# Slot-mean prologue moved ahead of the first statistics, PSUM copies of the transposes shared by two engines, and two waits merged

## The reference

```python
xn = layernorm(x)
# first branch: a gated scan along the tokens
w, k = (xn @ Wp + bp) split;  u = xn @ Wu + bu
gate = sigmoid(w);  s = gate * (s * tanh(k) + u) + (1 - gate) * s   # per token
attn = s_all @ Wo + bo
# second branch: 64 slots
slot_mean = mean of the 64 rows of slot_init (same for all tokens)
h = gelu(concat(xn, slot_mean) @ w1 + b1)
logits = (h @ w2 + b2) / (abs(tau) + 0.1)
alpha = softmax over the 8 largest of 64 logits, scattered back to 64
slot_input = alpha^T @ xn, summed over all tokens   # then a GRU, an attention
slot_values = ...                                   # over 64 slots, a layernorm
out = x + attn + (alpha @ slot_values) @ wo + bo
```

## Time and profile before

| | us |
|---|---|
| median of two runs | 1833.52 (1829.3 and 1837.74) |
| the profiled execution | 1837.19 |
| its span, from the slowest core's first to last instruction (core 6) | 1835.6 |
| spans of the eight cores | 1795.5 to 1835.6 |
| PE busy on core 6 | 1543.7 (84%) |
| DVE busy | 751.2 (41%) |
| ACT busy | 568.3 (31%) |

### The profile page before, as it was taken

One profiled execution on the slowest core, in us unless ns is written; L12 is line 12 of the kernel. 1 busy time (PEld: TensorE's weight loads), 2 busy tenths in 40 slices (PEclk: granted clock), 3 DMA queues, 4 the chain that ended last, 5 costly groups with the idle time before them and its releaser, 6 DMA issues.

```text
span 1835.6 us, 21069 instructions; the slowest of 8 cores (1795.5 to 1835.6 us)
## 1 busy us (share of the span) xinstructions
PE 1543.7 (84%) x7221; PEld 677.0 (37%) x7221; DVE 751.2 (41%) x1359; ACT 568.3 (31%) x926; POOL 26.9 (1%) x54
## 2 busy tenths in 40 slices
PE   0198999999999999999999899898844369999998
PEld 0044444444444444444444444444311123333333
DVE  0235444464554645546455464554501112222222
ACT  0252424244253352523525235252101121111110
POOL 0100000000000000000000000000011000000000
PEclk9999878899999999989989999999956669989898
DMA  9622020202202022021230302201199345545545
GB/s 152 152 46 92 1 92 1 92 2 91 92 1 92 24 69 92 1 92 37 57 92 1 92 34 60 92 1 47 53 151 168 60 128 207 202 184 192 198 184 206
DMA packets 42680, 166.52 MB, mean 91 GB/s; under 512 B 4290, under 2 KB 5458, under 8 KB 41682
## 3 DMA queue, kind: packets, MB, share of 16 engines
q1 hardware_dynamic: 36178, 134.29, 21.1%
q0 software_dynamic: 6400, 30.89, 10.2%
HBM read 128.68 MB, written 67.11 MB: 107 GB/s over the span
## 4 chain that ended last, share of the span: by engine, by line
PE 72%; DMA 10%; DVE 9%; issue 4%; DVEq 3%; ACT 2%; ACTq 0%; SPq 0%; POOL 0%; POOLq 0%
PE psA L1042 7%; PE psA L437 6%; PE psC L449 6%; PE psC L442 6%; PE psA L442 6%; PE psB L449 6%; PE psB L437 6%; PE psA L511 4%; PE psA L299 4%; PE psC L1042 3%; PE psB L1042 3%; PE psB L511 3%; DMA sb_bq_c<-bq_pk 2%; DVEq L102 2%; DMA sb_WT<-Wih_pk 2%
## 5 line engine op out<-in xcount | busy, mean ns | idle before, releaser
L19 ACT ACT_TABLE_LOAD x83 | 106.5, 1283 | 402.0 <-PE psA L511 398.2
L481 DVE SCALAR_TENSOR_TENSOR sb_a_sb<-sb_g_sb,sb_s_sb 128x512 f32<-128x512 f32 x128 | 88.6, 692 | 290.3 <-PE psB L449 157.2
L493 DVE TENSOR_TENSOR_SCAN sb_ys_bf<-sb_a_sb,sb_ys_bf,sb_b_sb 128x512 bf16<-128x512 f32 x120 | 154.1, 1284 | 8.9
L1042 PE MATMUL psA<-sb_wo_sb,sb_z_f 128*128 128x512 bf16 x512 | 138.6, 432 | 20.5 <-ACT sb_z_f L1011 18.8
L1057 DVE TENSOR_TENSOR sb_prd<-psA,sb_prd 128x1024 f32<-128x1024 f32 x32 | 39.2, 1224 | 258.6 <-DMA sb_prd<-out 171.1
L437 PE MATMUL psA<-sb_xn_f,sb_Wp_sb 128*128 128x512 bf16 x512 | 125.8, 390 | 0.0
L299 PE MATMUL psA<-sb_Wo_sb,sb_ys_bf 128*128 128x512 bf16 x512 | 121.3, 386 | 4.7 <-DVE sb_x_sl L327 4.7
L442 PE MATMUL psC<-sb_xn_f,sb_Wp_sb 128*128 128x512 bf16 x512 | 124.0, 386 | 0.0
L442 PE MATMUL psA<-sb_xn_f,sb_Wp_sb 128*128 128x512 bf16 x512 | 124.0, 386 | 0.0
L437 PE MATMUL psB<-sb_xn_f,sb_Wp_sb 128*128 128x512 bf16 x512 | 124.0, 386 | 0.0
L449 PE MATMUL psB<-sb_xn_f,sb_Wu_sb 128*128 128x512 bf16 x512 | 124.0, 386 | 0.0
(11 more groups left out here) (224 smaller groups left out, 1900.3 us busy)
## 6 DMA issues: line engine op xcount, KB each, us to landing
sb_x_sl<-x SPq DMA_DIRECT2D x32, 1024.0 KB, 7.4
out<-sb_x_sl SPq DMA_DIRECT2D x32, 1024.0 KB, 4.1
sb_prd<-out SPq DMA_DIRECT2D x16, 2048.0 KB, 10.5
out<-sb_prd SPq DMA_DIRECT2D x32, 1024.0 KB, 4.6
sb_WT<-Wih_pk POOLq DMA_DIRECT2D x12, 512.0 KB, 8.7
sb_whh_pp<-Whh_pk POOLq DMA_DIRECT2D x12, 512.0 KB, 8.6
sb_Wp_sb<-Wp_pk POOLq DMA_DIRECT2D x1, 4096.0 KB, 31.5
sb_Wu_sb<-Wu_pk POOLq DMA_DIRECT2D x1, 2048.0 KB, 37.8
```

The lines of the kernel that those rows point to most:

```text
L19: return eng.add_instruction(mybir.InstLoadActFuncSet(name=eng.bass.get_next_instruction_name(), act_func_set_id=idx, ins=[], outs=[]))
L481: P.op("ve", lambda v, pp=pp: v.scalar_tensor_tensor(t.a_sb[:], t.g_sb[:, pp, :], -2.0, t.s2_sb[:, pp, :], ALU.mult, ALU.mult))
L493: P.op("ve", lambda v, j=j, init=init: v.tensor_tensor_scan(t.ys_bf[:, j, :], t.a_sb[:], t.b_sb[:], init, ALU.mult, ALU.add), inc="sve", e ...
L1042: P.op("pe", lambda e, i=i, f=f, k=k, ps=ps, p2=p2: e.matmul(ps[:, f * 512:(f + 1) * 512], t.z_f[:, p2 % 2, k, i * 128:(i + 1) * 128], t.w ...
```

## The change

It has four parts.

1. The whole block for the slot mean (with its eight loads, and the three weight loads behind it) moves from behind `ln_apply(0)` to ahead of `stats_tile(0, ...)`. On DVE it so stands before `var_chain(0)`; on PE its place is the same.
2. In `xn_transposes` the blocks with odd `k` are copied by ACT with an Identity activation, those with even `k` still by DVE. PE waits for the last block of each engine.
3. In `wku_loop` the event `wk` is gone: ACT waits for `wku`, all 24 matmuls of the round, before its two sigmoids. DVE drops its own wait for `wku`.
4. In `h_logits` PE waits for the last of the four gelus before the first of the small matmuls; it waited for each of them in turn.

```diff
 (the block of L597 to L649, unchanged, now stands ahead of stats_tile)
...
-            P.wait("ve", ("xnT", ph, k))
+            eng = "ve" if k % 2 == 0 else "se"
+            P.wait(eng, ("xnT", ph, k))
             if ph >= 1 and k < 2:
-                P.wait("ve", ("wku", ph - 1, ND - 1))
-                P.wait("ve", ("hmm", ph - 1, NH - 1))
-            P.op("ve", lambda v, k=k, psT=psT: v.tensor_copy(
-                t.xn_f[:, k, :], psT[:, 0:Tp]), inc="sve", event=("xnf", ph, k))
+                P.wait(eng, ("wku", ph - 1, ND - 1))
+                P.wait(eng, ("hmm", ph - 1, NH - 1))
+            if k % 2 == 0:
+                P.op("ve", lambda v, k=k, psT=psT: v.tensor_copy(
+                    t.xn_f[:, k, :], psT[:, 0:Tp]), inc="sve",
+                    event=("xnf", ph, k))
+            else:
+                P.op("se", lambda s, k=k, psT=psT: s.activation(
+                    t.xn_f[:, k, :], psT[:, 0:Tp], AF.Identity), inc="sse",
+                    event=("xnf", ph, k))
...
     def wku_loop(ph):
         P.wait("pe", ("xnf", ph, ND - 1))
+        P.wait("pe", ("xnf", ph, ND - 2))
...
-                    t.xn_f[:, k, :], start=(k == 0), stop=(k == ND - 1)),
-                    inc="spe" if last else None,
-                    event=("wk", ph, j) if last else None)
+                    t.xn_f[:, k, :], start=(k == 0), stop=(k == ND - 1)))
...
-            P.wait("se", ("wk", ph, j))
+            P.wait("se", ("wku", ph, j))
...
             P.wait("ve", ("gs", ph, j))
-            P.wait("ve", ("wku", ph, j))
...
     def h_logits(ph):
         P.wait("pe", ("xnf", ph, ND - 1))
+        P.wait("pe", ("xnf", ph, ND - 2))
...
+        P.wait("pe", ("hf", ph, NH - 1))
         pe_claim("C0")
         for i in range(TPT):
             for kh in range(NH):
-                if i == 0:
-                    P.wait("pe", ("hf", ph, kh))
```

More of the change, by code:

```diff
@@ L206, in build_walk @@
         out=t.bo_tot[:], in_=t.bo1_r[:]), "sg", event=("botot",))
+    P.wait_all_dma("pe", ("cload",), "sx")
+    P.wait_all_dma("pe", ("wload",), "sg")
+    pe_claim("T0")
+    for k in range(ND):
+        P.op("pe", lambda e, k=k: e.transpose(
+            t.psT0[:, k * 64:(k + 1) * 64],
+            t.s0_bf[0:64, k * 128:(k + 1) * 128], t.ident[0:64, 0:64]),
+            inc="spe" if k == ND - 1 else None,
+            event=("s0T",) if k == ND - 1 else None)
+    P.wait("ve", ("s0T",))
+    for k in range(ND):
+        P.op("ve", lambda v, k=k: v.tensor_copy(
+            t.si0f[:, k, :], t.psT0[:, k * 64:(k + 1) * 64]),
+            inc="sve" if k == ND - 1 else None,
+            event=("si0f",) if k == ND - 1 else None)
@@ new lines, in build_walk @@
+    release("T0", ("si0f",))
+    P.drain("ve")
+    for k in range(ND):
+        P.op("ve", lambda v, k=k: v.reduce_sum(
+            t.sm_f[:, k:k + 1], t.si0f[:, k, :], axis=AX.X))
+    P.drain("ve")
+    P.op("ve", lambda v: v.tensor_scalar(t.sm_fb[:], t.sm_f[:], 1.0 / 64.0, None,
+                                         ALU.mult), inc="sve", event=("smf",))
+    regs4 = ["A0", "A1", "B0", "B1"]
+    pe_claim(*regs4)
+    ps4 = [psH[r] for r in regs4]
+    for k in range(ND):
+        if k >= 2:
+            P.wait("gp", ("smwk", k - 2))
+        P.dma("gp", lambda g, k=k: g.dma_start(
+            out=t.w1s[:, k % 2, :],
+            in_=t.i_w1[1024 + k * 128:1024 + (k + 1) * 128, :]), "sg",
+            event=("w1s", k))
+        P.wait("pe", ("w1s", k))
+        if k == 0:
+            P.wait("pe", ("smf",))
+        for jh in range(NH):
+            P.op("pe", lambda e, jh=jh, k=k: e.matmul(
+                ps4[jh][:, 0:1], t.w1s[:, k % 2, jh * 128:(jh + 1) * 128],
+                t.sm_fb[:, k:k + 1], start=(k == 0), stop=(k == ND - 1)),
+                inc="spe" if jh == NH - 1 else None,
+                event=("smwk", k) if jh == NH - 1 else None)
@@ L208, in stats_tile @@
+    P.wait("ve", ("smwk", ND - 1))
+    for jh in range(NH):
+        P.op("ve", lambda v, jh=jh: v.tensor_add(
+            t.bias_h[:, jh:jh + 1], t.b1_c[:, jh:jh + 1], ps4[jh][:, 0:1]),
+            inc="sve" if jh == NH - 1 else None,
+            event=("biash",) if jh == NH - 1 else None)
+    for r in regs4:
+        release(r, ("biash",))
+    for i, fn in enumerate(gload2):
+        P.dma("gp", fn, "sg", event=("wload2",) if i == len(gload2) - 1 else None)
     def stats_tile(ph, i):
@@ L440, in wku_loop @@
             for k in range(ND):
-                last = (k == ND - 1)
                 P.op("pe", lambda e, j=j, k=k, psk=psk: e.matmul(
                     psk, t.Wp_sb[:, k, 1024 + j * 128:1024 + (j + 1) * 128],
-                    t.xn_f[:, k, :], start=(k == 0), stop=(k == ND - 1)),
-                    inc="spe" if last else None,
-                    event=("wk", ph, j) if last else None)
+                    t.xn_f[:, k, :], start=(k == 0), stop=(k == ND - 1)))
             for k in range(ND):
@@ L596, in build_walk @@
     ln_apply(0)
[L598 to L649, removed]
     for ph in range(NPH + 1):
```

## The result

The changed kernel takes 1860.97 us (median), against 1835.78 us for the kernel before in the same comparison. The ratio is 1.018, with an interval of 1.013 to 1.022: slower by 1.8%, as forecast, and at the border of what counts as within 2%. The forecast time was 1867. In three of the eleven executions of the changed kernel one die ran at a lower granted clock and the time was 1974 to 2076 us; the ratio leaves such executions of either kernel out.

The account below looks back on a forecast made before the run. PE, busy 84% of the span, was taken as the bound, with DVE ending its wait before tile 3. Terms 18.2 + 9.6 + 1.8 + 6.3 - 2.0 gave +33.9 us, hence 1867 us; 8-in-10 range 1849 to 1884.

Parts of the forecast that it names:

- The late gates: In `wku_loop`, later sigmoids delay DVE's last round and so tile 3 of `wo_block`: 1.4 us in 13 phases, 18.2 us.
- The copies: In `xn_transposes`, the T1 chain goes through the slower ACT: 0.6 us a phase, 9.6 us in all (7 to 13.4).
- the faster reaction of PE to ACT: In `xn_transposes`, PE starts 0.14 us after ACT ends against 0.25 us after DVE's addition, lowering the price of ACT's copies.
- The gelus: In `h_logits`, three more small matmuls follow the wait for gelu 3: 0.11 us a phase, 1.8 us in all.
- The prologue: Before phase 0, slot-mean block and statistics change places without overlapping: a gain of 2 us (bounds 0 and 5).
- The clock: From slot matmuls to first L511, a longer pause makes 3 of 4 full-speed phases lose the clock: 6.3 us (0 to 16).
- the longer pause: Slot matmuls to first L511 gets some 0.6 us longer, given as the reason that more phases lose the full clock.
- The sum: For core 6: 18.2 + 9.6 + 1.8 + 6.3 - 2.0 = +33.9 us, 1867.4 against the median, 1.8% slower.
- The low-clock phases don't come back: Rival: without core 6's two slow phases the slowest core resembles core 1, 1810 + 42 = 1852 us; chance 0.12.
- the trace agrees, with 12 falls in 16: Before the first L511, 12 of core 6's 16 groups were slow, taken to support that transposes don't count as busy time.

Follow-up runs that it names:

- the gates alone: The kernel before with only both sigmoids made to wait for all three matmul groups of the round; ratio 1.010, median span 1833.8 us.
- part 1 alone: The kernel before with only the slot-mean block moved ahead of the statistics; one profiled execution, median span 1810.2 us.
- the copies alone: The kernel before with only the odd blocks of the transposes copied by ACT; ratio 1.010, median span 1834.4 us.
- an altered order: The changed kernel with DVE running `ln_apply` of the next phase behind the addition of tile 1, not the last scan; ratio 1.013 to the kernel before.
- the pause filled: The changed kernel with 13 extra unread matmuls a phase between the transposes; ratio 1.011 to the kernel before, median span 1831.9 us.

## Why the prediction was right, and what in it was not

**The late gates: right.** 1.4 us a phase forecast, 1.48 measured (22.2 us over 15 phases; 21.9 with the gates alone). The path was the one named: last sigmoids, DVE's last round, `ln_apply`, the addition of tile 0, tile 3. The regions of round 7 and the last scan held nobody. What was too small is the count: 13 phases were taken, because two were at low clock on core 6. The profiled run of the changed kernel had no such phases, and all 15 paid. Not foreseen was that the longer wait before tile 3 can itself be a place for falls: 19 with the gates alone, none in the changed kernel.

**The copies: right in mechanism, a little low.** 0.6 us a phase, between 0.4 and 0.84; measured 0.72 to 0.73. The copy took less than the nearest row: 597 ns, where 629 ns had been taken from rows 8. From the groups by line and shape:

```profile
L480 ACT ACTIVATE sb_xn_f<-psT 128x512 bf16<-128x512 bf16 x64 | 38.2, 597 | 291.2 <-PE psT L465 291.2
```

What was overrated is the faster reaction of PE to ACT, for which up to 0.11 us a block had been deducted. The 0.25 us of the forecast was measured behind an addition. Behind DVE's copy of a block PE started 0.15 us later (645.25 + 0.42 to 645.82), behind ACT's 0.14. A pair so takes 1.22 us, 0.16 more than before, of the 0.18 us by which ACT's copy is longer than DVE's 420 ns; the first pair takes 1.33 us, 0.13 more. Behind the last block PE even reacts later to ACT (0.35 us to the first L511, against 0.25 to DVE), which makes 0.27 us: 0.13 + 0.16 + 0.16 + 0.27 = 0.72.

**The gelus: low.** 0.11 us forecast, 0.19 measured, within the bound of 0.2. That the wait would be a second place for falls was not foreseen.

**The prologue: right.** -2 us forecast, -2.7 us measured between the medians of the cores (-2.0 with part 1 alone), for the reason given: the chains change places.

**The clock: right in sign, low in size, and its reason not shown.** 6.3 us in the sum. Between the six cores of before and the eight of the changed kernel, pass 1 grew by 45.4 us; less 20.9 for its 14 waits before tile 3, 15 x 0.73 = 11.0 and 2.9 this leaves 10.6 us for the clock. All but 2 of 120 pauses lose it, where 86 had lost it before. The forecast's reason was the longer pause. The runs don't bear out that length alone decides: with a shortest pause of 6.80 us there were 58, 68, 86, 92 and 117 falls, with one of 7.53 us 80, 82, 117 and 118. With the copies alone the clock cost 15 us, with the gates alone 2. Rows of the kernel before could not give such a number.

**The sum was made on the wrong core.** These terms are 22.2 + 11.0 + 2.9 + 10.6 - 2.7 = 44.0 us for a core without the low clock, and the median span moved by 42.8 (46.1 without the cores 6 and 7 of before). As the clock's term is a remainder, this only says that nothing outside pass 1 and the prologue changed much. My sum said 33.9 for core 6 and arrived near the measured time, because core 6 had some 25 us on its account that did not return. What came about is the rival *The low-clock phases don't come back*: it said 1810 + 42 = 1852, and the slowest core took 1856.6. It was given 0.12. So the direction was earned by the mechanisms, but that the ratio came out at 1.018, on the forecast's side of 2%, is in part luck. The kernel before ran from 1815 to 1845 us in this comparison; in the three later ones its medians were 1821 to 1825 us, and against those 1861 us would be 2.0 to 2.2% more. Stretches at 0.81 probably made the difference, but only one execution of this comparison shows its stretches. Why they come is open: of the fourteen profiled executions here, the kernel before is the only one with them, and nothing was tried on it.

The Trainium skill's sentence on transposes ("TensorE: Matmul & The Clock Gate", Part 4, PE-mode transpose) says that transposes don't count as busy time for the clock as other matmuls do. The runs fit this but don't test it: with the transposes alone the clock fell in 58 to 118 of 120 pauses of 6.8 us and more, and with ordinary matmuls between them it stayed up in all 120, in both kernels. But the extra matmuls also filled time in which PE was idle, so that the share of the transposes is not told apart from that of the idle time. The forecast's "the trace agrees, with 12 falls in 16" says no more either.

## What to carry to other kernels

Before a wait is moved or merged, follow the waiting engine's own program order to the next thing that PE needs from it. Here 1.4 us in front of `ln_apply` arrived in full at tile 3, and an altered order, without touching the gates, took away more than half of the waits that they cost. Splitting copies over two engines by PSUM region puts every second region on the slower engine; count the cycle of one region, not the busy time of the copiers. And when PE pauses once a phase, price each change with the clock held up as well as free: 13 matmuls a phase that nobody reads gave 1.5% here, and showed what the other edits cost by themselves.

## What the hardware showed that I had not expected

- The clock can eat a gain whole. Taking away 8 us of waits before tile 3 gave a ratio of 1.000, with half-clock time up from 246 to 295 us a core and the shortest pause unchanged.
- The place of the falls moves. With the pause filled, the changed kernel's clock fell 53 times at the first groups of `wku_loop`, behind a wait of 1.07 us and 20 small matmuls; the kernel before has a wait of 0.88 us there, three small matmuls earlier, and none. With the gates alone it fell 19 times at tile 3, behind a wait of 2 us. In dense matmuls a fall cost 1.7 us at either place.
- ACT's copy of a bf16 block of 128x512 from PSUM takes 597 ns, against 629 ns for an f32 source.
- In thirteen of the fourteen profiled executions here, all eight cores ran their dense matmuls without a stretch at 0.81. In the profiled one of the kernel before two cores of one die had two each.
